# A turned gate projection, per-head scaling of the output, and written-out engine sequences in a fused attention and expert layer

## What is computed

```python
xn = _layernorm(x)
qkv = xn @ w_qkv.T                       # q and gate: 16 heads of 128, k and v: 4 heads of 128
q = _layernorm(q, q_norm_w, q_norm_b)    # k the same with its own weights; then the rotation by position
scores = einsum('bhqd,bhkd->bhqk', q, k) / sqrt(128)      # causal
out = einsum('bhqk,bhkd->bhqd', softmax(scores), v)
out = out.reshape(1, 2048, 2048) * sigmoid(gate)
attention = out @ w_o.T
h = square(relu(einsum('nc,ecd->ned', xn, w_fc)))         # 8 experts, the two best of each row count
x + attention + combined einsum('ned,edc->nec', h, w_proj)
```

## Time and profile before

| | us |
|---|---|
| median of three runs | 1535.41 |
| lowest and highest | 1534.39, 1536.03 |
| span of the profiled execution | 1534.4 |
| the execution's own time beside the span: the run that reads the same | 1534.39 |
| idle time of TensorE in the span, by busy time | 32.9 |

### The profile page before, as it was taken

One profiled execution on the slowest core, in us unless ns is written; L12 is line 12 of the kernel. 1 busy time (PEld: TensorE's weight loads), 2 busy tenths in 40 slices (PEclk: granted clock), 3 DMA queues, 4 the chain that ended last, 5 costly groups with the idle time before them and its releaser, 6 DMA issues.

```text
span 1534.4 us, 29715 instructions
## 1 busy us (share of the span) xinstructions
PE 1501.5 (98%) x10589; PEld 1380.6 (90%) x10589; DVE 1304.1 (85%) x3037; ACT 1152.4 (75%) x3017; POOL 364.7 (24%) x502
## 2 busy tenths in 40 slices
PE   5999999999999999999999999999999999999998
PEld 3889999999989999999998999999999899999998
DVE  8999888888998888788799888877879888887788
ACT  4777776778887778777878777777787877768765
POOL 6545434420322111111042211111104221011010
PEclk8999999999999999999999999999999999999999
DMA  5411011011121111111111110111022211001013
GB/s 175 163 38 46 28 43 51 30 53 49 60 60 49 35 42 49 39 39 39 59 59 59 40 49 12 49 39 39 20 74 63 60 49 42 18 22 31 9 50 124
DMA packets 45124, 78.82 MB, mean 51 GB/s; under 512 B 4784, under 2 KB 30896, under 8 KB 44784
## 3 DMA queue, kind: packets, MB, share of 16 engines
q1 hardware_dynamic: 41232, 66.65, 14.2%
q0 software_dynamic: 3744, 10.26, 1.9%
HBM read 58.25 MB, written 24.72 MB: 54 GB/s over the span
## 4 chain that ended last, share of the span: by engine, by line
PE 86%; DVE 8%; ACT 3%; issue 2%; DMA 1%; POOL 1%; SPq 0%; DVEq 0%; ACTq 0%; POOLq 0%
PE bank L1392 45%; PE o_bank L1392 22%; PE pt_bank L1467 14%; PE bank L1445 2%; PE bank L1488 2%; DVE t_same L1266 1%; DVE pT_lo L1316 1%; ACT probs L1017 1%; DVE bank L1299 1%; DVE t_same L1262 1%; ACT pT_hi L1036 1%; DVE neg_chunk_max L1302 1%; DVE sumsq L1234 1%; DVE t_same L1250 1%; PE bank L1509 1%
## 5 line engine op out<-in xcount | busy, mean ns | idle before, releaser
L1017 ACT ACTIVATE probs<-bank,neg_max 128x512 f32<-128x512 f32 (+3 forms) x640 | 400.0, 635 | 100.8 <-DVE neg_max L1309 61.5
L1316 DVE TENSOR_TENSOR pT_lo<-pt_bank,pT_hi 128x512 fp32r<-128x512 f32 (+1 forms) x576 | 369.5, 655 | 87.4 <-ACT pT_hi L1036 82.9
L1036 ACT ACTIVATE pT_hi<-pt_bank 128x512 fp32r<-128x512 f32 (+1 forms) x576 | 326.7, 579 | 119.7 <-PE o_bank L1392 59.3
L1392 PE MATMUL o_bank<-pT_hi,v_hi 128*128 128x256 f32 x1088 | 331.8, 305 | 0.4 <-DVE pT_lo L1316 0.3
L1467 PE MATMUL pt_bank<-ident_rows,probs 128*128 128x128 f32 x2176 | 313.3, 273 | 2.5 <-DVE pT_lo L1316 1.5
L1392 PE MATMUL o_bank<-pT_hi,v_lo 128*128 128x256 f32 x1088 | 307.2, 282 | 0.0
L1392 PE MATMUL o_bank<-pT_lo,v_hi 128*128 128x256 f32 x1088 | 306.6, 282 | 0.0
L1302 DVE TENSOR_REDUCE neg_chunk_max<-bank 128x1 f32<-128x512 f32 (+1 forms) x384 | 244.8, 651 | 58.7 <-PE bank L1392 58.1
L1467 PEld LDWEIGHTS pt_bank<-ident_rows,probs 128*128 128x128 f32 x2176 | 252.1, 140 | 25.2 <-DVE pT_lo L1316 3.8
L1392 PE MATMUL bank<-kT_hi,qT_hi 128*128 128x512 f32 (+3 forms) x640 | 242.7, 379 | 0.7 <-ACT probs L1017 0.6
L1392 PE MATMUL bank<-kT_hi,qT_lo 128*128 128x512 f32 (+3 forms) x640 | 231.2, 361 | 0.0
(11 more groups left out here) (167 smaller groups left out, 2852.1 us busy)
## 6 DMA issues: line engine op xcount, KB each, us to landing
norm_rows<-kept_tables SPq DMA_DIRECT2D x24, 384.0 KB, 3.1
made_tables<-kept_tables SPq DMA_DIRECT2D x24, 384.0 KB, 3.0
kept_tables<-made_tables SPq DMA_DIRECT2D x16, 384.0 KB, 2.5
rows<-xs SPq DMA_DIRECT2D x23, 258.0 KB, 2.7
expert_raw<-in_w_fc SPq DMA_DIRECT2D x23, 256.0 KB, 3.0
expert_raw<-in_w_proj SPq DMA_DIRECT2D x23, 256.0 KB, 2.7
xs<-in_x_fill SPq DMA_DIRECT2D x11, 516.0 KB, 5.4
w_raw<-in_w_in SPq DMA_DIRECT2D x7, 640.0 KB, 4.2
```

The costliest lines, as they stand in the source:

```text
L1017: act.activation(probs[:, u, h % 2, first:first + width], bank("scores", g, t, h, c)[:, 0:width], ACT.Exp, bias=neg_max[:, u, h % 2:h % 2 ...
L1036: act.activation(pT_hi[:, n % PT_RING, 0:width], pt_bank[n % 2][:, 0:width], ACT.Copy)\
L1316: dve.tensor_tensor(pT_lo[:, n % PT_RING, 0:width], pt_bank[n % 2][:, 0:width], pT_hi[:, n % PT_RING, 0:width].bitcast(F32), ALU.subtract) ...
L1392: ins = pe.matmul(out_ap, s, m, start=(start and done == 1), stop=(stop and done == last))
```

## The change

1. The gate is projected turned. `G` now works for a pair of tiles and one head: the head's 128 gate columns of the weights are stationary and 256 rows of xn stream, so that the gate stands as features by rows. `GT` and its four transposes a tile are gone. `tanh` is done per pair of tiles and head into `gateT`.
2. The gate isn't scaled by the row sums any more, and `gate_scale` and `o_take` are gone. `og0` on VectorE makes (gateT + 1) times `o_bank` in one instruction for each half of a tile. As the sums are then still missing, `OUT` gives each head's product in columns of its own (two heads in a bank), `o_scale` on ScalarE multiplies each of the four by its reciprocal per row, and `out_add` on GpSimd adds each to `acc`. The last tile is scaled and added by VectorE (`out_last`).
3. `norm` moves from VectorE to ScalarE, with a shift that GpSimd makes in two more small steps; the centring of the weights moves to ScalarE (five instructions a part).
4. The planner goes; the sequence of every engine stands in the text as letters, one for a queue (`ORDERS`), and the PSUM bank of each product in `BANKS`.

New waits: `og0` waits for `out_add` of the tile before (its `oT` is read there), `pv` of the next tile for `og0`, `tanh` for `og0` of the tile before its pair, and `comb` for `out_add` of its tile.

```diff
-FREED_BY = {"Q": "q_take", "KV": "v_lo", "G": "tanh", "QT": "q_lo", "KT": "k_lo", "GT": "og", "OUT": "out_add",
+FREED_BY = {"Q": "q_take", "KV": "v_lo", "G": "tanh", "QT": "q_lo", "KT": "k_lo", "OUT": "o_scale",
...
+    "pool": ("ACBCCECEECEEEEEEEFEEFEEEFFEEFEFEEEFFEEEDFDFEFEEFEDEEDFFDDDFDFEEEDEEEFFDDDDDDDEFFEEEFDDEEFFEFDDDDDDEEDDDE"
...
+BANKS = ("40243140301443240123401232102143014310120143031240310430420310143203412324102432012403412403142301023401"
...
+def engine_orders():
+    queues = program_queues()
+    engines, bank_of, prior, held = {}, {}, {}, {}
+    for engine, order in ORDERS.items():
+        rest = {letter: iter(queues[queue]) for letter, queue in QUEUES[engine].items()}
+        engines[engine] = [next(rest[letter]) for letter in order]
+    for step, b in zip((step for step in engines["pe"] if step[0] in FREED_BY), map(int, BANKS)):
+        bank_of[step], prior[step], held[b] = b, held.get(b), step
+    return engines, bank_of, prior
...
-        gate = sb("gate", [P, 2, QW])
+        gateT = sb("gateT", [P, HG, 2 * P])
...
+                    w.wait_ge(rstd_x_done, 4 * n + 1)
                     pool.tensor_tensor(x_rstd[:, tiles], x_var[:, tiles], minus_half[:, 0:last - first], ALU.pow)\
                         .then_inc(rstd_x_done, 1)
+                    w.wait_ge(rstd_x_done, 4 * n + 2)
+                    pool.tensor_tensor(x_shift[:, tiles], x_mv[:, tiles, 0], x_rstd[:, tiles], ALU.mult).then_inc(rstd_x_done, 1)
+                    w.wait_ge(rstd_x_done, 4 * n + 3)
+                    pool.tensor_scalar(x_shift[:, tiles], x_shift[:, tiles], -1.0, None, ALU.mult).then_inc(rstd_x_done, 1)
...
+                elif kind == "out_add":
+                    g, t, p = a
+                    n = number[step]
+                    w.wait_ge(o_scaled, number["o_scale", g, t, p])
+                    if n > 1:
+                        w.wait_ge(pool_added, n - 1)
+                    pool.tensor_tensor(acc[:, t, :], acc[:, t, :], oT[:, 256 * p:256 * p + 256], ALU.add).then_inc(pool_step, 1)
+                    w.wait_ge(pool_step, n)
+                    pool.tensor_tensor(acc[:, t, :], acc[:, t, :], o_rows[:, p], ALU.add).then_inc(pool_added, 1)
...
+                elif kind == "norm":
+                    first, last = X_PARTS[a[0]]
+                    w.wait_ge(rstd_x_done, 4 * a[0] + 4)
+                    for t in range(first, last):
+                        act.activation(xn[:, t, 0:C], acc[:, t, :], ACT.Identity, bias=x_shift[:, t:t + 1],
+                                       scale=x_rstd[:, t:t + 1]).then_inc(xn_done, 1)
...
+                    n = 2 * g + c
+                    w.wait_ge(mean_step, 2 * n + 2)
+                    for h in range(HG + 1):
+                        ins = act.activation(raw[:, h * D:(h + 1) * D], raw[:, h * D:(h + 1) * D], ACT.Identity,
+                                             bias=minus_mean[:, h:h + 1])
+                    ins.then_inc(centred, 1)
+                    w.wait_ge(centred, n + 1)
                     act.activation(w_hi[:, c, 0:GATE_AT], raw[:, 0:GATE_AT], ACT.Copy).then_inc(wq_hi_done, 1)
...
                 elif kind == "tanh":
...
-                    w.wait_ge(filled, fill["G", g, t])
...
-                    act.activation(gate[:, t % 2, :], bank("G", g, t)[:], ACT.Tanh, scale=0.5).then_inc(gate_done, 1)
+                    g, q, h = a
+                    n = g * T + 2 * q
+                    w.wait_ge(filled, fill["G", g, q, h])
+                    if n:
+                        w.wait_ge(o_gated, 2 * (n - 1) + h // 2 + 1)
+                    act.activation(gateT[:, h], bank("G", g, q, h)[:, 0:2 * P], ACT.Tanh, scale=0.5).then_inc(gate_done, 1)
...
-                elif kind == "gate_scale":
...
+                elif kind == "o_scale":
+                    g, t, p = a
                     n = g * T + t
+                    w.wait_ge(filled, fill["OUT", g, t, p])
                     w.wait_ge(inv_done, n + 1)
-                    w.wait_ge(gate_done, n + 1)
-                    for h in range(HG):
-                        gh, inv = gate[:, t % 2, h * D:(h + 1) * D], row_inv[:, h:h + 1]
-                        ins = act.activation(gh, gh, ACT.Identity, bias=inv, scale=inv)
-                    ins.then_inc(gated, 1)
+                    for i, rows_to in enumerate((oT[:, 256 * p:256 * p + 256], o_rows[:, p])):
+                        h = 2 * p + i
+                        ins = act.activation(rows_to, bank("OUT", g, t, p)[:, i * C:(i + 1) * C], ACT.Copy,
+                                             scale=row_inv[:, t % 2, h:h + 1])
+                    ins.then_inc(o_scaled, 1)
...
-                elif kind == "o_take":
+                elif kind == "og_hi":
                     g, t, p = a
...
-                    act.activation(oT[:, 256 * p:256 * p + 256], o_bank[:, 256 * p:256 * p + 256], ACT.Copy)\
-                        .then_inc(o_copied, 1)
-                elif kind == "og_hi":
...
+                    cols = slice(256 * p, 256 * p + 256)
+                    w.wait_ge(o_gated, 2 * (g * T + t) + p + 1)
                     act.activation(ogT_hi[:, cols], oT[:, cols], ACT.Copy).then_inc(og_hi_done, 1)
...
-                elif kind == "norm":
...
-                        dve.tensor_scalar(xn[:, t, 0:C], acc[:, t, :], x_mv[:, t, 0:1], x_rstd[:, t:t + 1],
-                                          ALU.subtract, ALU.mult).then_inc(xn_done, 1)
...
+                    w.wait_ge(centred, n)
...
+                    if i:
+                        w.wait_ge(inv_done, i)
                     dve.tensor_reduce(row_sum[:], chunk_sum[:, t % 2, :, 0:n], AX.X, ALU.add).then_inc(sum_step, 1)
                     w.wait_ge(sum_step, i + 1)
-                    w.wait_ge(gated, i)
-                    dve.reciprocal(row_inv[:], row_sum[:]).then_inc(inv_done, 1)
...
-                elif kind == "og":
...
-                    w.wait_ge(filled, fill["GT", g, t])
...
-                    dve.tensor_tensor(oT[:, cols], bank("GT", g, t)[:, cols], oT[:, cols], ALU.mult).then_inc(og_done, 1)
+                    if i >= 2:
+                        w.wait_ge(o_scaled, number["o_scale", *tile_before(g, t, 2), 1])
+                    dve.reciprocal(row_inv[:, t % 2], row_sum[:]).then_inc(inv_done, 1)
+                elif kind == "og0":
+                    g, t, p = a
+                    n, q = g * T + t, t // 2
+                    cols, tokens = slice(256 * p, 256 * p + 256), slice((t % 2) * P, (t % 2 + 1) * P)
+                    w.wait_ge(pv_done, number["pv", g, t, p, (t + 2) // 2 - 1])
+                    w.wait_ge(gate_done, number["tanh", g, q, 2 * p + 1])
+                    if n:
+                        w.wait_ge(pool_added, number["out_add", *tile_before(g, t), p])
+                    dve.scalar_tensor_tensor(oT[:, cols].rearrange("p (h q) -> p h q", h=2), gateT[:, 2 * p:2 * p + 2, tokens], 1.0,
+                                             o_bank[:, cols].rearrange("p (h q) -> p h q", h=2), ALU.add, ALU.mult).then_inc(o_gated, 1)
...
+                elif kind == "out_last":
+                    g, t, p = a
+                    w.wait_ge(filled, fill["OUT", g, t, p])
+                    w.wait_ge(inv_done, g * T + t + 1)
+                    w.wait_ge(pool_added, number["out_add", g - 1, t, 1])
                     w.wait_ge(acc_done, acc_before[step])
-                    dve.tensor_tensor(acc[:, t, :], bank("OUT", g, t)[:, 0:C], acc[:, t, :], ALU.add)\
-                        .then_inc(acc_done, 1)
+                    for i in range(2):
+                        h = 2 * p + i
+                        dve.scalar_tensor_tensor(acc[:, t, :], bank("OUT", g, t, p)[:, i * C:(i + 1) * C], row_inv[:, t % 2, h:h + 1],
+                                                 acc[:, t, :], ALU.mult, ALU.add).then_inc(acc_done, 1)
+                        w.wait_ge(acc_done, acc_number[step] - 1 + i)
...
+                    w.wait_ge(pool_added, number["out_add", G - 2 if t >= LATE_COMB else G - 1, t, 1])
...
-                elif kind in ("Q", "KV", "G"):
+                elif kind == "G":
+                    g, q, h = a
+                    tokens = slice(2 * q * P, 2 * (q + 1) * P)
+                    cols = slice(QW + 2 * D + h * D, QW + 2 * D + (h + 1) * D)
+                    w.wait_ge(wg_lo_done, 2 * g + 2)
+                    w.wait_ge(xT_lo_done, 2 * part_of(2 * q + 1) + 1)
+                    three(bank("G", g, q, h)[:, 0:2 * P], [(w_hi[:, c, cols], w_lo[:, c, cols]) for c in range(CT)],
+                          [(xT_hi[:, c, tokens], xT_lo[:, c, tokens]) for c in range(CT)]).then_inc(filled, 1)
+                elif kind in ("Q", "KV"):
                     g, t = a
                     tokens = slice(t * P, (t + 1) * P)
...
-                    w.wait_ge(wg_lo_done if kind == "G" else wq_lo_done, 2 * g + 2)
+                    cols = {"Q": slice(0, QW), "KV": slice(QW, QW + 2 * D)}[kind]
```

(21 more changed lines are left out.)

568 lines of the change are left out of this document (231 added, 337 removed), and 22 rows, old and new, of the table BEGIN.

## The result

The changed kernel takes 1554.4 us (median of 4 runs, 1553.85 to 1555.54) against 1535.2 for the kernel before: ratio 1.0126, 95% interval 1.0112 to 1.0141. It is 19 us slower, where 20 us faster was forecast. The profiled execution has a span of 1552.1 us.

The account below looks back on a forecast made before the run. TensorE, busy for 98% of the span, was taken as the bound, with chains between engines counting at both ends. Terms -24.4 + 5 + 2 - 1.4 - 2 = -20.8 us gave 1515 us; 8-in-10 range 1501 to 1528.

Parts of the forecast that it names:

- TensorE, middle: TensorE's work between start and end: GT gone -28.2 us, G in smaller matmuls +3.9, net -24.4 us.
- Rotation: Rotation between KV and its turn: 4.8 us of TensorE work to cover some 6.9 needed; +5 us (0 to +10).
- The third case: Rival: GpSimd's adds and VectorE lengthen each other, mostly felt in rotations; +10 us, to about 1524; chance 0.15.
- The slower rival: Rival: og0 waits too late for out_add of the tile before, delaying TensorE; 1546 at 0.25 us each; chance 0.07.
- ScalarE, GpSimd, VectorE operations: New operations: o_scale 0.49 us, adds 0.83, og0 0.417 to 0.481; busy time ScalarE +15 us, VectorE -10; no bound.
- Banks: OUT's PSUM bank: 126 fillings freed by two ScalarE copies, some too late for the next filling; +2 us (0 to +8).
- Start: Up to the first turn of q, put at 29.8 us with more TensorE work done by then; -1.4 us (-5 to +4).
- End: After the last pv: o_take leaves the chain, out_last adds, comb stands earlier on VectorE; -2 us (-3 to +1).

Follow-up runs that it names:

- tiny adds: Changed kernel with all 252 GpSimd adds on 8 columns instead of 256, the rest of each sum left out: 1519.8 us, ratio 0.9897.
- the runs that divide the adds: Changed kernel with only the 46 out_adds beside a rotation's last step on 8 columns: 1525.8 us; with only the other 80 so: 1552.2 us.
- The powers: Changed kernel with each GpSimd add replaced by a 128x2 power of about the same duration, nothing added to acc: 1522.8 us.
- the run with the rows out of oT: Changed kernel with o_scale writing the first head's rows where ogT_hi stands, og_hi waiting for out_add instead of og0: 1555.2 us.
- adds were held: Changed kernel with out_add, in 119 of 126 places, waiting until the rotation ahead has ended on VectorE: 1558.7 us, ratio 1.0149.
- Four runs: Changed kernel, x's second part first: 1561.8 us; 46 out_adds held, Q first: 1537.2; norm and centring on VectorE again, with tiny adds: 1527.9, with 46 held: 1541.2.
- two placements: Changed kernel with GpSimd's adds moved to VectorE ahead of og0: 1613.4 us; with scaling and adding on VectorE out of PSUM instead: 1601.2 us.

## Why the prediction was wrong

By its own steps:

- **TensorE, middle (-24.4): right.** All 10717 matmuls are there, 768 of them in G. Summing the distances between TensorE's instructions by shape, as the prediction did, and taking the sum from the time of the last matmul, leaves about 41 us more not worked after than before (57.7 and 98.6 us, with 0.23, 0.175, 0.12 and 0.11 us for 512, 384, 256 and 128 columns). The last matmul starts at 1531.5 before and 1548.3 after, 16.9 later, so the work itself fell by about 24.
- **Rotation (+5, 0 to +10): the step that failed.** It counted the shorter cover, which the tiny adds bear out in direction (TensorE's wait for t_same is 4.9 us, 2.5 above before), and it named adds near swap and rstd as its high end, in eight places, priced as time for which GpSimd is occupied. It did not look one step further in the same piece of order: in 45 of the 64 rotations an out_add stands directly behind rstd, and what runs on VectorE at that moment is the end of the rotation, which the adds lengthen. There they cost 16 us of waits for t_same (21.2 against 4.9 with tiny adds). The other 18 of the 34.6 us lie in other waits, 6.6 of them in that for the split of probabilities (pT_lo, 7.0 against 0.4); the runs that divide the adds tie most of the 34.6 to the same 46, but how the delay passes from the rotation to the other waits wasn't followed.
- **The third case, "VectorE and GpSimd get in each other's way", had the mechanism, with its size wrong.** It priced the overlap as 50 to 100 us of lengthening on VectorE of which a tenth reaches TensorE, +10, and gave it a chance of 0.15. Measured, VectorE's busy time grew by 37.7 us (1322.1 against 1284.4 with tiny adds), less than assumed, and the time by 31 to 35 us, eight to nine tenths of it. The tenth assumed that the overlap is spread over VectorE's work and meets its idle time. It isn't: it falls on the rotation, the one chain that the same prediction had just found 2 us short of cover. Counted by places, 46 out_adds at the measured 0.62 to 0.76 us each are +29 to +35, which puts 1515 at 1544 to 1550 and leaves 4 to 10 us that are the start and what the other 80 cost.
- **The rows that bore on it were read, but with the wrong neighbour.** In tile (3, 2) L1250 took 0.81 us, and the prediction put that down to rstd. The row of GpSimd just ahead of it was not shown; its last product ends at 1173.20, 0.26 us after L1250 has begun:

```profile
1171.13 2.06 POOL L878 TENSOR_TENSOR t_swap<-qk_raw,norm_rows 128x256 f32<-128x256 f32 x4 [6.50 <-ACT t_same L986]
```

Sorted over the whole trace of before, L1250 takes 0.68 us alone (19 cases) and 0.68 behind a running rstd (28), but 0.80 to 0.81 where the end of swap's last product runs beside it (16). rstd lasts 1.61 to 1.65 us, instead of mostly about 1.19, in the seven cases in which L1250 was running when it began. So in this tile swap held up L1250, and L1250 held up rstd. No row of before shows the three-operand instruction beside a 128x256 operation of GpSimd, and the estimate took its size (0.2 to 0.4 us) from milder pairs; beside a 128x256 add the 0.35 us instruction takes 0.69 to 0.77 on average. The Trainium skill, "SBUF — State Buffer", section "Who interferes with whom", says that VectorE with two inputs from SBUF contends with a GpSimd instruction that reads SBUF, that the shared pair is an exclusive lock, and, of VectorE's modes that use two ports, that whoever issues first has it for the whole instruction while the other fully blocks. If that held here, an estimate from the rows is 0.35 and up to an add's 0.76 us, 1.11; (3, 4) shows 0.81 to 0.90 for the four that grew, inside it. The powers differ from what the page says of instructions that read SBUF: both their inputs are in SBUF, they last as long as an add, and 101 rotation instructions beside them grew by nothing.
- **The slower rival (og0 waits for out_add): wrong for this kernel** (1.8 us of waits, and the run with the rows out of oT is unchanged), though the kernel did come out slower. It was waiting behind: once adds were held, og0 waited 32.2 us.
- **ScalarE, GpSimd, VectorE operations: right** in durations (0.480, 0.774 to 0.830, 0.414). ScalarE's busy time fell by 6 us where +15 was taken, and VectorE's, without the overlap, by 20 where -10 was. The copy with one scale per row took 480 ns, where the one without had taken 392.
- **Banks (+2): too much.** TensorE waits for o_scale (o_rows) 0.3 us in all.
- **Start (-1.4): wrong by 4 to 5 us.** The first turn of q came at 30.81, inside the bound of 32; but counted by distances up to 120 us, the kernel before has some 30 us not worked and the one with tiny adds 3.2 more. The sum for the start also used prices that don't hold there: the first matmuls of 512 columns in the trace of before stand 0.43 us apart, not 0.23. Four runs failed to get it back; with norm and centring on VectorE again the start is 6 us worse, so by these runs their move isn't the cause. It stays open.
- **End (-2): nearly nothing.** From 1500 us to the last matmul about 3 us were not worked before and 1.7 after; from the last matmul's start to the end of the span it is 2.9 before and 3.8 after.

Without the adds' cost the change takes 1519.8 us, 4.8 above the forecast; the start's miss is about as large, and the other terms nearly cancel. With it, one term that was priced at 0 to 10 us and measured 34.6 decides the sign.

## What to carry to other kernels

Moving work to an idle engine is free in its own queue only. Before placing it, ask which instructions of its neighbour run at the same time, whether both read their inputs from SBUF, and whether those lie on the chain with the least cover: 46 out_adds of 1.6 us each, on an engine 36% busy, cost 29 us, and 80 others cost 2 to 6. To hold such work back can pay, but only after whatever waits for it has been given a place of its own: held alone +4 us, given a place alone nothing, both together -12, and -19 when only the ones that collide are held, all against the changed kernel.

## What the runs showed of the hardware

- A three-operand VectorE instruction of 128x128 with both inputs in SBUF takes 0.35 us alone and 0.69 to 0.77 on average beside a 128x256 add on GpSimd. The adds grow too, from 0.74 to 0.83 us and from 0.76 to 0.93 on average, single ones to 1.8. A VectorE instruction with one input in PSUM doesn't grow (684 and 684 ns).
- Which of the two is held up depends on which began first: in the kernel before, rstd on GpSimd lasts 1.61 to 1.65 instead of mostly about 1.19 us where L1250 of VectorE was already running (7 cases), and L1250 lasts its usual 0.68 where rstd was (28).
- One input in SBUF can be enough: the step that makes the variance (L1239 of before, 128x5, one input, in SBUF) takes 0.17 us alone and 0.28 on average, 0.68 at most, beside swap's products (48 cases).
- A GpSimd power of 128x2 that lasts as long as the add (0.756 us) and also reads SBUF lengthens nothing (means of 346 and 348 ns in 101 cases). The length of the neighbour's instruction is therefore not what counts. That it is how much the neighbour reads would fit the adds on 8 columns (means of 347 and 346 ns beside them), but they are also short and the power is another operation, so these runs don't settle it.
- VectorE at 85% had little room in two placements: 111 and 121 us more on it cost 94 and 81.
